# The down stages of a fused attention and feed-forward kernel: another order of banks, additions and next tokens' work

## What is computed

```
x = x + tanh(g_xattn[0]) * xattn(layernorm(x), ctx, ctx, Wq, Wk, Wv, Wo)   # 32 heads, 8 key heads of 32
xt = layernorm(x)
up   = xt @ W_up.T            # F = 2752
gate = silu(xt @ W_gate.T)
x = x + tanh(g_ffn[0]) * ((gate * up) @ W_down.T)
```

## Time and profile before

| | us |
|---|---|
| median of the runs | 2066.15 |
| lowest and highest | 2064.88, 2068.79 |
| profiled execution, own time | 2068.12 |
| its span, first to last instruction | 2066.3 |

### The profile page before, as it was taken

One profiled execution on the slowest core, in us unless ns is written; L12 is line 12 of the kernel. 1 busy time (PEld: TensorE's weight loads), 2 busy tenths in 40 slices (PEclk: granted clock), 3 DMA queues, 4 the chain that ended last, 5 costly groups with the idle time before them and its releaser, 6 DMA issues.

```text
span 2066.3 us, 30111 instructions
## 1 busy us (share of the span) xinstructions
PE 2010.1 (97%) x9800; PEld 1684.0 (81%) x9800; DVE 1223.2 (59%) x1818; ACT 917.0 (44%) x2218; POOL 658.3 (32%) x601
## 2 busy tenths in 40 slices
PE   7999999999999999999999999999999999999999
PEld 5888788788888778888888887777888888888877
DVE  6867676776787664545454556575545454434455
ACT  4873584496378243333332444343333333333334
POOL 2340342143244534544543111022544544300000
PEclk9999999999999999999999999999999999999999
DMA  5225215322424222212222665663212221246666
GB/s 192 81 79 194 88 57 187 119 77 102 166 75 157 86 82 92 91 70 82 91 87 77 218 215 200 222 210 139 92 68 84 91 85 67 103 156 211 211 231 222
DMA packets 90602, 266.65 MB, mean 129 GB/s; under 512 B 11136, under 2 KB 37248, under 8 KB 85120
## 3 DMA queue, kind: packets, MB, share of 16 engines
q1 hardware_dynamic: 90496, 265.33, 37.3%
HBM read 221.25 MB, written 39.32 MB: 126 GB/s over the span
## 4 chain that ended last, share of the span: by engine, by line
PE 87%; DVE 6%; ACT 3%; issue 3%; DMA 1%; SPq 0%; DVEq 0%; ACTq 0%
PE ps L1459 27%; PE ps L1461 27%; PE ps L1460 27%; PE ps L1509 2%; ACT pb L780 1%; PE ps L1500 1%; PE ps L1501 1%; DMA x<-in_x 1%; DVE kb_h L1096 1%; PE ps L1554 1%; DVE xo L1361 1%; PE ps L1660 1%; PE ps L1671 1%; DVE dl L1046 1%; DVE wr_l L1046 0%
## 5 line engine op out<-in xcount | busy, mean ns | idle before, releaser
L1459 PE MATMUL ps<-xop_h,w_h 128*128 128x512 f32 x1208 | 473.1, 392 | 2.1 <-issue 2.1
L1461 PE MATMUL ps<-xop_h,w_l 128*128 128x512 f32 x1208 | 471.0, 390 | 0.0
L1460 PE MATMUL ps<-xop_l,w_h 128*128 128x512 f32 x1208 | 470.8, 390 | 0.0
L1459 PE MATMUL ps<-dh,hh 128*128 128x512 f32 x672 | 265.7, 395 | 6.4 <-DVE xo L1361 5.1
L1459 PEld LDWEIGHTS ps<-xop_h,w_h 128*128 128x128 f32 x1208 | 227.6, 188 | 48.9 <-issue 2.5
L1461 PEld LDWEIGHTS ps<-xop_h,w_l 128*128 128x128 f32 x1208 | 227.3, 188 | 47.4
L1460 PEld LDWEIGHTS ps<-xop_l,w_h 128*128 128x128 f32 x1208 | 227.6, 188 | 46.5
L1460 PE MATMUL ps<-dl,hh 128*128 128x512 f32 x672 | 262.5, 391 | 0.0
L1461 PE MATMUL ps<-dh,hl 128*128 128x512 f32 x672 | 262.5, 391 | 0.0
L1046 DVE TENSOR_TENSOR w_l<-fraw,w_h 128x512 fp32r<-128x512 f32 x130 | 130.0, 1000 | 213.8 <-ACT w_h L723 213.8
L723 ACT ACTIVATE w_h<-fs 128x512 fp32r<-128x512 f32 x168 | 105.7, 633 | 285.0 <-PE ps L1461 280.4
(11 more groups left out here) (159 smaller groups left out, 3872.2 us busy)
## 6 DMA issues: line engine op xcount, KB each, us to landing
dr<-in_wd SPq DMA_DIRECT2D x132, 512.0 KB, 4.2
fraw<-in_wf SPq DMA_DIRECT2D x42, 1024.0 KB, 5.3
wc_raw<-in_wc SPq DMA_DIRECT2D x44, 512.0 KB, 4.3
hd<-hb SPq DMA_DIRECT2D x42, 512.0 KB, 2.9
hr<-hd SPq DMA_DIRECT2D x84, 192.0 KB, 3.1
wr_raw<-in_wr SPq DMA_DIRECT2D x24, 512.0 KB, 3.4
x<-in_x SPq DMA_DIRECT2D x5, 2048.0 KB, 8.5
x1d<-x SPq DMA_DIRECT2D x16, 512.0 KB, 4.2
```

Source lines behind the costliest of these rows:

```text
L1459: pe.matmul(out, w_hi_, m_h, start=first, stop=False, skip_group_check=goes_on)
L1460: pe.matmul(out, w_hi_, m_l, start=False, stop=False, skip_group_check=goes_on)
L1461: return pe.matmul(out, w_lo_, m_h, start=False, stop=last, skip_group_check=goes_on)
```

## The change

- Pass 2 uses banks 0, 1, 2, 4 in place of 0, 4, 3, 5, so its four banks wait for the first four additions of pass 1. The first quad of half 1 now shares banks 0, 1 and 2 with pass 2 and gets two more waits, before its second and third product.
- `add_ffn` takes a list of banks. At the start of a pass VectorE's order is: split of step 0, additions 0 and 1, split of step 1, the other additions, split of step 2. Ahead of half 1 each of the first four weight splits is followed by one addition.
- Pair 1 is transposed in steps 3 and 4 of pass 1, and split behind the splits of step 5.
- Normalisations: sequence pair 0 behind step 7 of pass 0 (was behind 8, with pair 1), pair 1 behind the token splits of pass 0, pair 2 behind step 5 and pair 1's token splits in pass 1 (was behind 8), pair 3 before the last step of pass 1 (was behind step 8 of pass 2).
- Steps 3 to 8 are written out in place of a loop of two rounds, on all three engines.

```diff
-Y_BANK = ((0, 1, 2, 4, 3, 5), (0, 1, 2, 4, 3, 5), (0, 4, 3, 5))
-Y_BEFORE = (None, (1, 2, 3, 4, 5, 6), (1, 4, 5, 6))
+Y_BANK = ((0, 1, 2, 4, 3, 5), (0, 1, 2, 4, 3, 5), (0, 1, 2, 4))
+Y_BEFORE = (None, (1, 2, 3, 4, 5, 6), (1, 2, 3, 4))
...
                     if p > 0:
                         for f in range(RING):
                             down_hi(s, p, f, 0)
+                    for f in range(3, 6):
+                        down_hi(s, p, f, 0)
                     if more and p == 1:
                         pair_tokens_hi(s + 1, 1)
-                    with act.Fori(0, 2) as i:
-                        for f in range(3, 6):
-                            down_hi(s, p, f, i)
-                    for f in range(9, 12):
+                    for f in range(6, 12):
                         down_hi(s, p, f, 0)
...
-            def add_ffn(s, p):
+            def add_ffn(s, p, parts):
                 tiles = 8 * s + FIRST[p] + TILES[p]
                 dve.wait_ge(xo_in, 16 * tiles)
-                for idx in range(NH * TILES[p]):
+                for idx in parts:
...
                     for j in range(PROD):
                         weight_lo(s, 0, 0, j)
-                    add_ffn(s - 1, PASSES - 1)
+                        if j < NH * TILES[PASSES - 1]:
+                            add_ffn(s - 1, PASSES - 1, (j,))
                     quad(s, 0, 0)
...
                     if p > 0:
                         down_lo(s, p, 0, 0)
+                        add_ffn(s, p - 1, (0, 1))
                         down_lo(s, p, 1, 0)
-                        add_ffn(s, p - 1)
+                        add_ffn(s, p - 1, range(2, NH * TILES[p - 1]))
                         down_lo(s, p, 2, 0)
-                    if more and p == 1:
-                        pair_tokens_lo(s + 1, 1)
-                    with dve.Fori(0, 2) as i:
-                        for f in range(3, 6):
-                            down_lo(s, p, f, i)
-                    if more:
-                        for t in ((0, 1), (2,), (3,))[p]:
-                            normalise2(s + 1, t)
-                    for f in range(9, 12):
+                    for f in range(3, 12):
                         down_lo(s, p, f, 0)
+                        if more and p == 1 and f == 5:
+                            pair_tokens_lo(s + 1, 1)
+                            normalise2(s + 1, 2)
+                        elif more and p == 0 and f == 7:
+                            normalise2(s + 1, 0)
                     if more:
                         pair_tokens_lo(s + 1, (0, 2, 3)[p])
+                    if more and p == 0:
+                        normalise2(s + 1, 1)
                     with dve.Fori(0, 3) as i:
                         for f in range(12, 15):
                             down_lo(s, p, f, i)
+                    if more and p == 1:
+                        normalise2(s + 1, 3)
                     down_lo(s, p, FT - 1, 0)
...
                 product(s, c, i, 0, 0, 0, bx, True, True)
                 if not begin:
                     pe.wait_ge(comb, combs(s, c, i, 0) - 5)
+                elif s > 0:
+                    pe.wait_ge(y_free, y_count(s - 1, PASSES - 1, 2))
                 product(s, c, i, 1, 1, 1, by, True, True)
+                if begin and s > 0:
+                    pe.wait_ge(y_free, y_count(s - 1, PASSES - 1, 3))
...
-                    for f in range(RING):
+                    for f in range(9):
                         t = None
-                        if more and p == 1 and f == 0:
-                            t = {"pair": 1, 1: (0,), 2: (1,), 3: (2,), 4: (3,), 5: (4,)}
-                        elif more and p == 1 and f == 1:
-                            t = {"pair": 1, 0: (5,), 1: (6,)}
+                        if more and p == 1 and f == 3:
+                            t = {"pair": 1, 0: (0,), 1: (1,), 2: (2,), 3: (3,)}
+                        elif more and p == 1 and f == 4:
+                            t = {"pair": 1, 0: (4,), 1: (5,), 2: (6,)}
                         down_step(s, p, f, 0, t)
-                    with pe.Fori(0, 2) as i:
-                        for f in range(3, 6):
-                            down_step(s, p, f, i)
```

More of the change, by code:

```diff
@@ L1450, in _ @@
                             down_lo(s, p, f, i)
+                    if more and p == 1:
+                        normalise2(s + 1, 3)
                     down_lo(s, p, FT - 1, 0)
-            add_ffn(NS - 1, PASSES - 1)
+            add_ffn(NS - 1, PASSES - 1, range(NH * TILES[PASSES - 1]))
         @block.tensor
```

## The result

| | before | after |
|---|---|---|
| median, us | 2066.77 | 2055.70 |
| lowest and highest, us | 2064.88, 2068.79 | 2054.44, 2056.78 |
| profiled execution, us | 2068.12 | 2055.99 |
| its span, us | 2066.3 | 2054.2 |

The ratio is 0.9947, with a 95% interval of 0.9934 to 0.9959: 11.1 us faster. The forecast was 13.7 us off 2066.15, so 2052.5. The time came out 3.2 us above it, inside the range.

The account below looks back on a forecast made before the run. TensorE, busy 2010.1 of 2066.3 us, was taken as the bound, so only its waits and half-clock stretches could be won. Terms summed to 13.9, less 0.2 gives 13.7, off 2066.15: 2052.5 us, range 2050 to 2059.

Parts of the forecast that it names:

- Part 1: Start of pass 1, both halves: additions among the splits leave 0.5 of 1.02 us lost, 0.5 gained in each half.
- Part 2: Start of pass 2: new banks leave 0.4 us; 1.6 gained in each half, plus 1.7 for the clock in half 0.
- the ring: Pass 2, step 5: load, copy and subtraction chain, costed at nothing; split ends 1348.3 to 1349.8, wanted at 1349.9.
- Part 3: Pass 1, pair 1's transposes moved to steps 3 and 4: third set's wait of 1.50 us becomes 0.48, gain 1.0.
- Part 4: Moved normalisations: pair 3's third set in pass 2 gains 1.5 us, 1.1 left, plus 1.6 for the clock.
- all four collisions: End of pass 1: GpSimd's four pair sums slow VectorE by at most 4.4 us; it finishes by 1334.1, costing 0 to 0.3.
- Rival B: GpSimd's sums catch VectorE in all three new places, with one clock fall: 4.5 us, so 2057; chance 0.09.
- Part 5: Start of half 1: the "issue" wait is for an addition; moving it gains 2.2 us, and 1.7 for the clock.
- Part 6: Steps 3 to 8 written out: 0 gain, as the pass holding both loops has no gap.
- The clock: Three 3.4 us half-clock stretches behind gaps in the down stages would go, at about 1.7 us each.
- Rival A: The clock falls as often as now, behind the gaps that stay: about 5.0 us, so 2057.5; chance 0.13.
- From profile to median: The profiled 2068.12 us lies 2.0 above the median 2066.15, so 2054.4 for the profiled execution became 2052.5.

Follow-up runs that it names:

- after_again: The changed kernel (after) run once more with no edit: 2055.36 us, ratio 0.9944 to the kernel before.
- u5_adds_last: After with the four additions ahead of half 1 put back behind all seven weight splits: 2058.98 us, ratio 0.9960 to the kernel before.

## Why the prediction was right, point by point

- **What bounds the kernel.** Right: the gain stands in the waits named in the earlier trace rows and in the clock, and but for the wait at step 5 nothing else changed: the rest of the down stages is 896 us in every trace without a fall.
- **Part 1**, 0.5 left: 0.37 measured. VectorE's rows are as worked out, additions 0 and 1, the two splits, then the four others:

```profile
1236.95 1.41 DVE L1360 SCALAR_TENSOR_TENSOR xo<-ps,tg,xo 128x512 f32<-128x512 f32 x2 [1.87 <-PE ps L1763]
...
1238.74 1.22 DVE L1045 TENSOR_TENSOR dl<-dr,dh 128x1024 fp32r<-128x1024 f32 x1
1239.87 2.72 DVE L1360 SCALAR_TENSOR_TENSOR xo<-ps,tg,xo 128x512 f32<-128x512 f32 x4
```

- **Part 2**, 0.4 left: 0.24. The failed step is the ring behind it: "I cost it at nothing; it has 0 to 1 us of cover." It took 1.07, 1.07 and 0 in half 0 of after, after_again and u5_adds_last, where the prediction's bounds allowed none: VectorE's `dl` for step 5 ended at 1350.6 in after, not between 1348.3 and 1349.8. The weights could be copied only 7.2 us after their issue, beyond the 6.0 of the earlier trace rows. I had looked at the landing times, and not at what else was in flight with that very load. The bunch was there before as well; the stall that went had been its cover.
- **Part 3**, 0.64 left, and no wait at step 6: both so.
- **Part 4**, 1.1 left for pair 3: 0.54, 1.05 in after_again, and 2.36 in u5_adds_last, though nothing before it in that kernel differs from after. So the 1.1 is right only as a middle value. The cause named, ScalarE's `dh` held by step 11's load, is what u5_adds_last's row shows (1.71 us idle for `dr`). The end of pass 1 went as worked out, VectorE done with step 0's `dl` at 1332.9 where the bound gave 1334.1 with all four collisions. The rows show one collision on `dl` (2.30 in place of 1.22), and `hl` ahead of it took 1.19 in place of 0.42:

```profile
1330.62 2.30 DVE L1045 TENSOR_TENSOR dl<-dr,dh 128x1024 fp32r<-128x1024 f32 x1
1333.67 1.41 DVE L1360 SCALAR_TENSOR_TENSOR xo<-ps,tg,xo 128x512 f32<-128x512 f32 x2 [0.74 <-PE ps L1763]
```

- **Rival B.** Steps 6 and 12 had no wait: the splits slipped in ahead of GpSimd, as in the earlier trace rows. It falls.
- **Part 5**, 2.2 from the gap: 2.2 between the two profiles, 1.9 in u5_adds_last. Its idle time was 1.7 to 2.9 in the five traces that have it, so this one varies.
- **Part 6**, nothing: 1.0007 [0.9997, 1.0017].
- **The clock**, 5.0 in the sum: mis-sized, and the main reason for the medians' miss. I read the three falls of one trace as a property of three gaps. The traces of before have 2.3 on average, of about 1.5 us each and not 1.7, which makes 3.3 us; the mean clocks of all executions give two falls. Rival A had the right idea, that the fall isn't tied to the gap alone, and the wrong side: falls can also be absent from before. It is half true.
- **From profile to median.** The three runs' 2066.15 lay 1.2 below the median of the 73, 2067.4. The miss of 3.2 us is thus about 1.2 from there, 1.7 from the clock, and the rest is scatter. The waits don't add to it, and in that there is luck: the 1.07 of the ring is paid by parts 1, 2 and 4, which left less than forecast.

## To carry to other kernels

When a stall goes, whatever waited in its shadow is next: look at the one load in flight at that place, at what its queue issued just before and behind it, and not at a landing time taken over the whole pass. Put each piece of work where its first user wants it: the additions by the order in which banks are closed and asked for, and a long store one piece at a time between the loads of a ring. And count clock falls over several executions; a single trace can hold three or none for the same code.

## What the runs showed of the hardware

**The clock behind a gap.** Identical code with gaps of 0.5 to 2.9 us idle showed 3, 1 and 3 stretches of 3.4 us at 1.2 GHz (granted clock 0.50) in its down stages, and the same code with one loop written out none. Each began inside a gap or at most 1.5 us behind its end, and cost about 1.5 us. Which gap brings one stays open.

**A load beside a bunch of stores.** The same 512 KB load could be used 6.2 to 7.2 us after its issue with three stores just ahead of it in SyncE's queue, and 4.0 to 4.6 with one.

**Who gets the port of GpSimd and VectorE.** GpSimd's first sum behind pair 2's normalisation, and VectorE's work beside it, from the timeline of after:

```profile
1264.75 4.28 POOL L658 TENSOR_TENSOR ts<-xs 128x512 f32<-128x512 f32 x1 [58.61 <-DVE xs L1238]
...
1264.59 0.55 DVE L1045 TENSOR_TENSOR hl<-hr,hh 128x384 fp32r<-128x384 f32 x1
1265.05 1.22 DVE L1045 TENSOR_TENSOR dl<-dr,dh 128x1024 fp32r<-128x1024 f32 x1
...
1266.66 1.22 DVE L1045 TENSOR_TENSOR dl<-dr,dh 128x1024 fp32r<-128x1024 f32 x1
```

Four VectorE instructions in a row, to 1267.88, kept their usual times, and the sum stood there for 4.28 us. Only after VectorE had been idle (0.73 before 1268.61) did its own instructions grow, `dl` to 2.12. "SBUF — State Buffer" in the Trainium skill, section "SBUF: two separate sides", says that whichever starts first holds the shared ports for its whole instruction; the trace agrees. It shows besides that a waiting GpSimd is passed over by VectorE instructions that follow on each other without a pause. In pass 0, behind step 11, a sum stood for 4.28 us in the same way (from 1196.40). I take this to be why the earlier normalisations cost nothing at steps 6 and 12; no run changed it alone.
